# Two row-maximum tiles in one PSUM bank, bf16 halves of the maxima split before the transpose, and a later reciprocal in an attention kernel

## What is computed

```python
std_logits = jnp.einsum('bhqd,bhkd->bhqk', q, k) * scale
geo_logits = jnp.einsum('bqhi,bkhi->bhqk', read_lines, J_write) * inc_scale.reshape(1, H, 1, 1)
mask = jnp.triu(jnp.ones((T, T), dtype=bool), k=1)
std_attn = jax.nn.softmax(jnp.where(mask, neg, std_logits), axis=-1)
std_out = jnp.einsum('bhqk,bhkd->bqhd', std_attn, v).reshape(B, T, D)
geo_attn = jax.nn.softmax(jnp.where(mask, neg, geo_logits), axis=-1)
geo_out = jnp.einsum('bhqk,bkhd->bqhd', geo_attn, geo_v).reshape(B, T, D)
combined = (1.0 - gate) * std_out + gate * geo_out
```

## Time and profile before

| | us |
|---|---|
| median of 3 runs | 1853.19 |
| lowest, highest | 1847.12, 1853.97 |
| profiled execution | 1854.49 |
| its span, first to last instruction | 1852.8 |

### The profile page before, as it was taken

One profiled execution on the slowest core, in us unless ns is written; L12 is line 12 of the kernel. 1 busy time (PEld: TensorE's weight loads), 2 busy tenths in 40 slices (PEclk: granted clock), 3 DMA queues, 4 the chain that ended last, 5 costly groups with the idle time before them and its releaser, 6 DMA issues. The chain is left out here.

```text
span 1852.8 us, 32056 instructions
## 1 busy us (share of the span) xinstructions
PE 1638.3 (88%) x11809; PEld 583.7 (32%) x11809; DVE 1078.2 (58%) x2557; ACT 1216.9 (66%) x1457; POOL 337.6 (18%) x479
## 2 busy tenths in 40 slices
PE   7896459998999999999969999999999856999998
PEld 4553212222222222222212222222222223655564
DVE  4775476666666666666646666676666214445433
ACT  3554407888888888889858888888988841112211
POOL 4332311111111111110202111111011113212000
PEclk9999658999999999999979999999999987999999
DMA  5664521221212212212121221211211014232000
GB/s 169 212 206 158 187 71 41 85 85 45 84 44 64 71 45 64 70 46 71 52 64 40 64 71 45 66 58 55 71 60 36 18 60 133 76 105 80 18 16 23
DMA packets 97372, 140.32 MB, mean 76 GB/s; under 512 B 8144, under 2 KB 66320, under 8 KB 95152
## 3 DMA queue, kind: packets, MB, share of 16 engines
q1 hardware_dynamic: 96000, 135.08, 22.2%
q0 software_dynamic: 624, 2.75, 0.5%
q10 hardware_dynamic: 576, 0.28, 0.1%
HBM read 81.96 MB, written 55.61 MB: 74 GB/s over the span
## 5 line engine op out<-in xcount | busy, mean ns | idle before, releaser
L1143 ACT ACTIVATE prob<-ex 128x1024 f32<-128x1024 f32 (+1 forms) x1152 | 1048.6, 979 | 219.2 <-PE ex L971 193.7
L1162 DVE TENSOR_REDUCE mp<-mx 128x1 f32<-128x512 f32 x768 | 491.9, 685 | 238.0 <-PE mx L1006 236.9
L1060 PE MATMUL pv<-prob,va 128*32 128x512 f32 (+3 forms) x5120 | 578.1, 542 | 0.4 <-POOL prob L943 0.4
L943 POOL TENSOR_SCALAR_AFFINE_SELECT prob<-prob 128x256 f32<-128x256 f32 (+1 forms) x384 | 186.4, 486 | 1060.2 <-ACT prob L1143 1055.0
L977 PE MATMUL ex<-dq,dk 34*128 34x512 bf16 (+7 forms) x2560 | 338.6, 350 | 27.2 <-ACT prob L1143 20.2
L1159 DVE CUSTOM_DVE_ANT_0 dull<-mx,mask_qk 128x384 f32<-128x384 f32 (+3 forms) x512 | 231.1, 489 | 132.4 <-PE mx L1006 129.4
L1006 PE MATMUL mx<-dk,dq 64*128 64x512 bf16 (+3 forms) x1280 | 257.1, 358 | 36.3 <-DVE mp L1162 21.4
L971 PE MATMUL ex<-gq,gk 38*128 38x512 bf16 (+3 forms) x1280 | 219.8, 356 | 37.8 <-ACT prob L1143 17.7
L971 PEld LDWEIGHTS ex<-gq,gk 38*128 38x128 bf16 x1280 | 56.7, 93 | 446.3 <-ACT prob L1143 383.6
L1490 ACT ACTIVATE sg<-pg 128x512 f32<-128x512 f32 x48 | 28.7, 597 | 247.5 <-PE pg L1430 247.4
L1060 PEld LDWEIGHTS pv<-prob,va 128*32 128x32 f32 x5120 | 114.4, 109 | 220.8 <-issue 195.4
(11 more groups left out here) (98 smaller groups left out, 904.2 us busy)
## 6 DMA issues: line engine op xcount, KB each, us to landing
values<-vn SPq DMA_DIRECT2D x32, 512.0 KB, 5.2
va<-values SPq DMA_DIRECT2D x16, 1024.0 KB, 18.1
raw<-on SPq DMA_DIRECT2D x64, 256.0 KB
parts_dot<-sp SPq DMA_DIRECT2D x32, 384.0 KB, 5.0
dq<-parts_dot SPq DMA_DIRECT2D x96, 128.0 KB
dk<-parts_dot SPq DMA_DIRECT2D x96, 128.0 KB
att<-raw SPq DMA_DIRECT2D x32, 256.0 KB
rr<-rden SPq DMA_DIRECT2D x32, 256.0 KB
```

Of the source, the lines that this page charges most:

```text
L943: g.affine_select(out=cut, in_=cut, compare_op=ALU.is_ge, fill=0.0, base=0, pattern=[[0, nb], [1, P]], channel_multiplier=-1).then_inc(mas ...
L1060: last = pe.matmul(pv[blk * VW:(blk + 1) * VW, CH - w:CH], sets[which]["v"][:, kb, blk * VW:(blk + 1) * VW], prob[UNIT_AT[s, j, kind] % NP ...
L1143: act.activation(prob[n % NPROB][:, :].rearrange("p (b c) -> p b c", b=2)[:, :, 0:w], ex[:, n % 2, :].rearrange("p (b c) -> p b c", b=2)[: ...
L1162: return v.tensor_reduce(out=to, in_=source, axis=AX.X, op=ALU.max)
```

## The change

Three edits. (1) Tiles on the diagonal whose widths add up to at most 512 share a bank, side by side: `MAX_IN[h]` is one bank pair, all its matmuls stand between the two kinds of scores, and PE and DVE exchange one semaphore a bank. There are 34 bank pairs instead of 40, and their order in the slots is new (diagonal tiles first in the early part). (2) In `turn`, DVE negates and reduces, rounds to bf16, and puts the rounded value and the rest side by side as columns before the transpose; behind it one cast to bf16 fills `mrow`, now 8 n rows of 128. Each pair of rows of `gq` or `dq` comes in one transfer. (3) `DEN_STEP` goes from 10 to 18, and the store of the first batch's inverses moves to the next item, behind the first `store`.

```diff
-DEN_STEP = 10
+DEN_STEP = 18
...
-    early = [f for qt in (1, 2) for f in fulls(qt)] + [cuts(qt, 3) for qt in (0, 1, 2)] + [cuts(2, 1)]
-    late = fulls(3)
...
+    early = [cuts((qt, 0), (qt, 2)) for qt in (0, 1)] + [cuts((0, 1), (1, 1))] + fulls(1) + [cuts((1, 3))] + fulls(2)
+    early += [cuts((0, 3)), cuts((2, 3)), cuts((2, 1), (3, 1)), cuts((2, 0), (2, 2))]
+    late = [cuts((3, 3))] + fulls(3) + [cuts((3, 0), (3, 2))]
...
-        mrow = [sb(f"mrow{p}", [4 * n, 2, P], BF16) for p, n in enumerate(PART_BLOCKS)]
+        top = [sb(f"top{p}", [P, 2, 2, n]) for p, n in enumerate(PART_BLOCKS)]
+        high = [sb(f"high{p}", [P, 2, 2, n], BF16) for p, n in enumerate(PART_BLOCKS)]
+        mrow = [sb(f"mrow{p}", [8 * n, P], BF16) for p, n in enumerate(PART_BLOCKS)]
...
-                    for i in range(2):
-                        geo = to["geo"][0][HALF * a + GEO_ROWS + i:HALF * a + GEO_ROWS + i + 1, cols]
-                        dot = to["dot"][0][HALF * a + DOT_MINOR + i:HALF * a + DOT_MINOR + i + 1, 1, cols]
-                        for kind, dst in ((GEO, geo), (DOT, dot)):
-                            at = (2 * kind + a) * n
-                            q.dma_start(dst.rearrange("p (k t) -> p k t", t=P),
-                                        mrow[part][at:at + n, i, :]).then_inc(m_in[part], 16)
+                    geo = to["geo"][0][HALF * a + GEO_ROWS:HALF * a + GEO_FULL, cols]
+                    dot = to["dot"][0][HALF * a + DOT_MINOR:HALF * a + DOT_MINOR + 2, 1, cols]
+                    for kind, dst in ((GEO, geo), (DOT, dot)):
+                        at = (2 * kind + a) * 2 * n
+                        q.dma_start(dst.rearrange("p (k t) -> p k t", t=P),
+                                    mrow[part][at:at + 2 * n, :])\
+                         .then_inc(m_in[part], 16)
...
+                    if it == PAIRS_OF_HEADS + 1:
+                        store_den(q, rden, 0, late)
...
-                if it == PAIRS_OF_HEADS:
-                    store_den(q, rden, 0, late)
...
+                at, last = 0, [None, None]
+                for u in MAX_IN[h]:
+                    qb, k0, w, _ = MAXT[u]
+                    for a in range(2):
+                        i = RING.place[h, a]
+                        if not at:
+                            bank_free(it, i)
+                        rows = slice(HALF * a, HALF * a + DOT_MAIN)
+                        last[a] = pe.matmul(mx[:, RING.bank[i], at:at + w], q_set[rows, 0, qb * P:(qb + 1) * P],
+                                            k_set[rows, 0, k0:k0 + w], start=True, stop=True)
+                        if u == MAX_IN[h][-1]:
+                            last[a].then_inc(mx_ready, 1)
+                    at += w
...
+                def highest(kind, maxima, rounded, done):
+                    v.tensor_reduce(out=top[part][:, kind, :, :], in_=mp[kind][:, :, blocks, :], axis=AX.X, op=ALU.max,
+                                    negate=True).then_inc(maxima, 1)
+                    v.wait_ge(maxima, nit + 1)
+                    v.tensor_copy(high[part][:, kind, :, :], top[part][:, kind, :, :]).then_inc(rounded, 1)
+                    v.wait_ge(rounded, nit + 1)
+                    v.tensor_copy(columns[:, kind, :, 0, :], high[part][:, kind, :, :])
+                    v.tensor_tensor(out=columns[:, kind, :, 1, :], in0=top[part][:, kind, :, :],
+                                    in1=high[part][:, kind, :, :], op=ALU.subtract).then_inc(done, 1)
...
-                src = mx[0:4 * n, RING.bank[i], 0:P]
-                v.tensor_copy(mrow[part][:, 0, :], src).then_inc(mrow_high[part], 1)
-                v.wait_ge(mrow_high[part], nit + 1)
-                v.tensor_tensor(out=mrow[part][:, 1, :], in0=src, in1=mrow[part][:, 0, :], op=ALU.subtract)\
-                 .then_inc(mrow_ready[part], 1)
+                v.tensor_copy(mrow[part][:, :], mx[0:8 * n, RING.bank[i], 0:P]).then_inc(mrow_ready[part], 1)
```

More of the change, by code:

```diff
@@ L146, in max_places @@
         at = at[:next(n for n, h in enumerate(at) if (TURN[part] - h) % NPV == 1) + 1]
[L147 to L151, removed]
+        assert len(at) == len(mine)
+        for h, us in zip(at, mine):
+            out[h] = us
+            assert sum(MAXT[u][2] for u in us) <= CH
+    assert sorted(u for us in out for u in us) == list(range(NMT))
     return out
@@ L156 @@
 LEAD = TURN[LATE] + 1
+NTILE = 2 * sum(1 for us in MAX_IN if us)
 class Ring:
@@ L798, in attend @@
         negm_ready = [sem(f"negm_ready{p}") for p in range(2)]
-        mrow_high = [sem(f"mrow_high{p}") for p in range(2)]
+        top_ready = [sem(f"top_ready{p}") for p in range(2)]
+        high_ready = [sem(f"high_ready{p}") for p in range(2)]
+        wx_top = [sem(f"wx_top{p}") for p in range(2)]
+        wx_high = [sem(f"wx_high{p}") for p in range(2)]
         mrow_ready = [sem(f"mrow_ready{p}") for p in range(2)]
@@ L992, in bank_free, with max_tiles_of @@
                     pe.wait_ge(mrow_ready[part], item_of(at, part) + 1)
-            def max_pair(it, to, u):
+            def max_tiles_of(it, to, h):
                 _, which, use = to
                 q_set, k_set = sets[which]["dot"]
-                if u == EARLY_FIRST:
+                if h == LEAD:
                     pe.wait_ge(sets[which]["dot_in"], (use + 1) * LOADS * 16)
[L1001 to L1007, removed]
+                at, last = 0, [None, None]
[11 more added lines that the diff above has]
+                    at += w
             def wide_pair(to, part, n, u):
@@ L1108, in prologue @@
                 for h in range(LEAD, NPV):
-                    for u in MAX_IN[h]:
-                        max_pair(-1, static(0), u)
+                    if MAX_IN[h]:
+                        max_tiles_of(-1, static(0), h)
                     if h in TURN:
@@ L1159, in row_max, with max_tiles_of @@
                     return v.tensor_tensor_reduce(
-                        out=dull[:, scrap, 0:w], in0=source, in1=mask_qk[:, CH - w:CH],
+                        out=scrap, in0=source, in1=mask_qk[:, CH - w:CH],
                         scale=1.0, scalar=3 * MASKED, op0=ALU.add, op1=ALU.max, accum_out=to)
                 return v.tensor_reduce(out=to, in_=source, axis=AX.X, op=ALU.max)
-            def max_pair(it, u):
-                qb, k0, w, on_diagonal = MAXT[u]
+            def max_tiles_of(it, h):
                 for a in range(2):
-                    i = RING.place[u, a]
+                    i = RING.place[h, a]
                     v.wait_ge(mx_ready, RING.ready(it, i))
-                    if on_diagonal:
-                        v.sem_inc(v_passed, 1)
-                    row_max(mx[:, RING.bank[i], 0:w], mp[DOT][:, a, qb, k0 // CH:k0 // CH + 1], w, on_diagonal,
-                            RING.bank[i]).then_inc(mx_free, 1)
+                    at = 0
+                    for u in MAX_IN[h]:
+                        qb, k0, w, on_diagonal = MAXT[u]
+                        if on_diagonal and not at:
+                            v.sem_inc(v_passed, 1)
+                        last = row_max(mx[:, RING.bank[i], at:at + w], mp[DOT][:, a, qb, k0 // CH:k0 // CH + 1], w,
+                                       on_diagonal, dull[:, RING.bank[i], at:at + w])
+                        at += w
+                    last.then_inc(mx_free, 1)
             def wide_pair(nit, part, n, u):
@@ L1193, in turn @@
                     v.wait_ge(wx_free[part], (nit + 1) * len(PART_TILES[part]))
-                    v.tensor_reduce(out=columns[:, GEO, :, :], in_=mp[GEO][:, :, blocks, :], axis=AX.X, op=ALU.max,
-                                    negate=True).then_inc(wx_rows[part], 1)
+                    highest(GEO, wx_top[part], wx_high[part], wx_rows[part])
                     v.wait_ge(wx_rows[part], nit + 1)
@@ L1257, in _ @@
             for h in range(LEAD, NPV):
-                for u in MAX_IN[h]:
-                    max_pair(-1, u)
+                if MAX_IN[h]:
+                    max_tiles_of(-1, h)
                 if h in TURN:
```

38 lines of the change are left out of this document (15 added, 23 removed).

## The result

The changed kernel takes **1822.76 us** (median of 4 runs, 1819.37 to 1828.30) against 1852.21 for the kernel before (4 runs): ratio 0.985, 95% interval 0.982 to 0.988. That is 29 us, 1.6%, faster. The forecast was 1854 us in a range of 1838 to 1868, so it is wrong: it said no change, and the kernel is faster than its range allows. The profiled execution took 1819.37 us; its span is 35.2 us shorter than that of before.

| stretch, by ACT's exponentials | before, us | after, us | difference | forecast |
|---|---|---|---|---|
| ahead of attention | 280.6 | 278.2 | -2.4 | 0 |
| item 0 | 77.02 | 74.59 | -2.4 | +1.3 |
| items 1 to 7 and 10 to 13 (11) | 826.83 | 819.40 | -7.4 | +8.8, and the clock's +9.1 |
| item 8 | 94.03 | 75.10 | -18.9 | -17.4 |
| item 9 | 73.94 | 73.83 | -0.1 | +1.8 |

The account below looks back on a forecast made before the run. Two DMA engines, working off operand loads with the maxima rows queued behind, were taken as the bound; terms of -8.3 us and +9.1 for the clock on the profiled 1854.49 gave 1855.3, as a median 1854 us, range 1838 to 1868.

Parts of the forecast that it names:

- The bound: Attention items: two DMA engines, loading operands with the maxima rows queued behind, set the length, about 74.8 us, after the change.
- Pairs: PE's slots in an attention item: maxima pairs side by side save 1.7 us of PE time, nearly all becoming waiting.
- The turn: Rounding before the transpose: PE waits 0.3 us in the late part, about nothing in the early; PE item length 72.6 us.
- SP's issue: Row transfers at an item's end: SP issues four instead of eight, 2.9 us less, but the wait is not there.
- Inversion: Item 8: the first inversion, moved to step 18, no longer waits for denominators; the item falls to 76.6 us, gain 17.4.
- The 1.0 us for the denominators' own transfers: Item 8: the denominators' transfers, on all 16 DMA engines, add about 1.0 us to its length.
- the +1.0 for item 9: Item 9: the store of the inverses goes ahead of its loads and adds 1.0 us.
- The rows: Item boundaries: merged row transfers put more packets on two busy engines, +0.8 us each (bounds 0 and 0.96), +10.4 over thirteen.
- The clock: Item boundaries: PE idles about 3 us, its clock falls at 7 more, 1.3 us each, +9.1 us (0 to +20).
- rival B: Item boundaries: rows spread as widely as now, gaps of 2.2 us, fewer clock falls; -14.3 us, 1839; chance 0.16.
- rival C: Item boundaries: rows land with their own issue, not behind the loads, so PE's 72.6 us holds; 1801 us; chance 0.04.
- A: Item boundaries: the clock falls at every one, +19.7 us instead of +9.1; 1865 us; chance 0.20.

## Why the prediction was wrong

**The bound: right.** An item was set by the two engines, as the earlier trace rows said, and is so after the change; the split store shows it by taking the bound away.

**Pairs, 1.7 us of PE an item, worth nothing in time: right.** The double slots are 1.97 to 1.99 us, and alone the edit changes the time by 0.1% (1853.48 for 1852.32), which is not clear of no change.

**The turn: mechanism right, the term too small, without effect.** The late part waits 0.42 us, 0.50 us in the slot, where I had 0.3; the early part costs 0.15 us where I had nothing. PE's length is 72.88 us for my 72.6; with the old turn it is 72.26, so the new one costs 0.62. None of it shows in the time while the DMA engines set the item.

**SP's issue, 2.9 us, worth nothing: right.** PE goes on 7.8 us behind the last issue.

**Inversion, -17.4 us: right.** It is -18.9 in the profile; alone, with the store that it moves, -16.8. The 1.0 us for the denominators' own transfers is there (item 8 is 75.10 beside 74.05 for item 7); the +1.0 for item 9 is not. I took all of the gain for the wait; the clock's fall at that stall, 23.9 us long, was in the length that I read, and I did not see it.

**The rows: the step that failed.** I took "then nothing, and 1.8 us later PE goes on" as fixed, the same for any number of transfers, and asked only what the packets add. The packets were right (48 on one engine, 0.71 us in place of 0.16), and the 0.8 us that I charged for them are 0.55. But the 1.8 us was not fixed: it was mostly the landings of eight transfers, 0.175 us each on a busy engine. With four of them the silence is 0.64. The sum at a boundary is -0.6 and not +0.8. The prediction mentioned that fewer completions go with it and gave that 0.16 us; it measures 1.1. The row that would have told it was there: eight packets in 0.16 us followed by a silence more than ten times as long is a fixed cost, and the next question, whether of the queue or of each transfer, I didn't ask. The counts of `m_in` in the trace of before, evenly 0.175 us apart, answer it: the first 0.66 us behind its packet, the eighth 1.20 us after the first.

The Trainium skill, "DMA: Bandwidth & Descriptors", section "Queues, rings and completion order", says that the increment of the semaphore is a strongly ordered write, which lands only after every earlier write of its engine. The order of the counts agrees with it (they come one by one, behind the data); their pace, 0.175 us, is from the runs. The Trainium skill, same title, "Rules for kernel authors", asks to coalesce many small transfers; here that paid 15 us, and nothing where PE was the bound. By the Trainium skill's section on why a DMA increments its semaphore by 16, which the prediction drew on, 2 x 12 rows go over two engines: the 12 KB on one engine in the window, half of the 96 packets, agree.

**The clock: the second step that failed, in number and in price.** I had eight falls at 1.3 us each, from gaps of 3 us. The gaps are 0.9 to 1.1 us at ordinary boundaries, because of the step above, and the clock fell at two boundaries, where the gaps were 3.40 and 2.52 us. The price was wrong as well, and by my own argument: where the DMA engines set the item, a slow stretch of PE only eats into the gap at the item's end. The kernel with eight transfers shows it. In windows at the start of its items 10 and 11 the clock is 0.5 and 1.0:

```profile
1039.00:1045.80 6.80, 6.66 (x50) 1.88 (x42) 3.58 (x6) 3.90 (x5) 2.89 (x6) 0.50 0.09 26
...
1112.70:1119.50 6.80, 6.34 (x74) 2.18 (x70) 4.62 (x8) 5.24 (x7) 3.10 (x7) 1.00 0.07 17
```

and ACT's starts of items 10, 11 and 12, with PE at the boundary from 10 to 11 and from 11 to 12:

```profile
1037.83 1.02 ACT L1148 ACTIVATE prob<-ex 128x1024 f32<-128x1024 f32 x1 [3.66 <-PE ex L974]
...
1113.11 1.02 ACT L1148 ACTIVATE prob<-ex 128x1024 f32<-128x1024 f32 x1 [1.01 <-PE ex L974]
...
1188.13 1.02 ACT L1148 ACTIVATE prob<-ex 128x1024 f32<-128x1024 f32 x1 [3.14 <-PE ex L974]
```

```profile
1112.68 0.39 PE L974 MATMUL ex<-gq,gk 38*128 38x512 bf16 x2
...
1187.70 0.39 PE L974 MATMUL ex<-gq,gk 38*128 38x512 bf16 x2 [2.07 <-issue]
```

The item with 6.8 us at the lower level lasts 75.28 us and ends without a gap; the next, at full speed, lasts 75.02 and ends with one of 2.07. A fall costs 0.3 us there, not 1.3; items 12 and 13 of the same kernel, with a fall and without, last 75.3 and 75.0 us. My +9.1 was a cost of PE added to an item that PE does not set.

**Corrected sum**, against the profiled execution of before: item 8 -18.9; item 0 -2.4; the other fourteen items -8.3 together, most of it from 0.6 us at a boundary; 5.5 us outside attention that the change doesn't explain: -35.1, for a difference of 35.1. Of item 0's 2.4 us the boundary's 0.6 is understood and the rest is not.

The chances: the time lies between rival B (1839) and rival C (1801). B had the direction, faster boundaries, and the wrong mechanism (rows spread over many engines); C, rows that land with their own issue, is refuted by the 7.8 us; its time, 1801, is what the store as two gives (1800), by the way that C describes. A, slower by the clock, is refuted by two falls at 15 boundaries. My bounds for the rows, 0 and +0.96 us, left out a gain, and no reason in the text excluded one.

**Open:** the kernels with eight transfers end their loads at 72.1 to 72.6 us into the item, and the changed kernel at 72.1. So of the 1.2 us an item between the changed kernel and the one with eight rows, 0.65 is the landings, and the rest, a later end of the loads by 0.5 us, was not taken apart; the landings account for some 9 of the 15.0 us. Nor did the runs tell why the clock fell after some gaps of 2 to 3 us and not after others (before, it held after 2.95 us; the changed kernel had a gap of 2.16 at 951.63 and no fall).

## What to carry to other kernels

Where a wait ends at the tail of a busy DMA queue, count the transfers that the semaphore waits for, not their bytes, and look at when each engine counts it up: here an even pace with no packets was a cost for each transfer, and merging them paid although the packets on the busy engines grew from 8 to 48. Before charging an engine for a slower clock or crediting it with shorter work, ask whether it sets the stretch at all; in the ordinary items here neither counted. And look which transfers run on two engines of sixteen: the output store, sent as two, was worth 23 us on the changed kernel, for an edit of a few lines.

## What the runs showed of the hardware

- Increments of a semaphore by successive small transfers on one DMA engine are 0.17 to 0.18 us apart, with one or twelve packets of 256 B in each. The packets themselves start 0.014 us apart in a transfer of 2 x 12 rows and 0.020 in eight of 1 x 12, where each is followed by a packet of 4 B. The first increment is 0.66 us behind its packet.
- A store of 2 x 64 rows runs on two engines (share 0.13); as two stores of 64 rows it left the two engines idle 7 us before the item's end, and the granted clock was 1.00 from 285 to 1400 us.
- In the attention stage of the changed kernel the granted clock was 0.50 for 6.8 and for 3.4 us at boundaries with a gap of 3.40 and 2.52 us, and for 3.4 us in the last item; in the kernel before, for 23.9 us around a stall of PE of 16.27 us. With the store as two, where PE has no gaps at the boundaries, it was never below 1.00 from 285 to 1400 us.
